# Routing and experts of a mixture-of-experts layer in one program block, with a slot table in two parts and rows scattered unscaled

## Reference, cut to what matters

```python
x = x + attn(layernorm(x))                      # 4096 tokens, DIM = 256
z = layernorm(x).reshape(-1, 256)
aff = z @ centroids.T                           # 8 experts
assign = argmax(aff, axis=1)                    # the expert of each token
alpha = sigmoid(aff[assign])
h = relu(layernorm(z, ln_g[e], ln_b[e]) @ w1[e].T + b1[e])   # 256 -> 1024, e = assign
y = z + h @ w2[e].T + b2[e]                     # 1024 -> 256
x = x + alpha * y + (1 - alpha) * z
```

## Time and profile before

| | |
|---|---|
| median of three executions | 949.11 us (947.34 to 951.23) |
| profiled execution | 948.4 us, its span 946.3 us |
| PE busy | 870.7 us, 92% of the span |
| DVE busy | 603.1 us, 64% |
| ACT busy | 534.9 us, 57% |
| POOL busy | 315.7 us, 33% |
| mean granted clock of TensorE | 0.972 |

### The profile page before, as it was taken

One profiled execution on the slowest core, in us unless ns is written; L12 is line 12 of the kernel. 1 busy time (PEld: TensorE's weight loads), 2 busy tenths in 40 slices (PEclk: granted clock), 3 DMA queues, 4 the chain that ended last, 5 costly groups with the idle time before them and its releaser, 6 DMA issues. The chain is left out here.

```text
span 946.3 us, 20352 instructions
## 1 busy us (share of the span) xinstructions
PE 870.7 (92%) x6606; PEld 517.7 (55%) x6655; DVE 603.1 (64%) x1111; ACT 534.9 (57%) x1338; POOL 315.7 (33%) x471
## 2 busy tenths in 40 slices
PE   7999869999999999999999989924999999999996
PEld 4555413333333333333333326613999999999996
DVE  5888999888888888888888306861333333323332
ACT  4667437777777877877777874661322232232221
POOL 9988644333332232232333321461111111111111
PEclk9999979999999999999999999966999999999998
DMA  7588442422521112222213207345666566656660
GB/s 263 168 255 248 143 130 96 157 69 69 169 69 47 48 49 65 69 68 69 69 56 105 90 1 240 122 165 204 211 192 210 194 197 193 219 185 199 199 212 6
DMA packets 55139, 130.68 MB, mean 138 GB/s; under 512 B 9753, under 2 KB 30874, under 8 KB 48794
## 3 DMA queue, kind: packets, MB, share of 16 engines
q1 hardware_dynamic: 49482, 108.19, 36.7%
q0 software_dynamic: 5584, 21.54, 6.0%
HBM read 101.21 MB, written 28.48 MB: 137 GB/s over the span
## 5 line engine op out<-in xcount | busy, mean ns | idle before, releaser
L802 ACT ACTIVATE arena<-ps_pair 128x512 f32<-128x512 f32 (+3 forms) x768 | 328.9, 494 | 102.2 <-PE ps_pair L1134 94.7
L891 DVE TENSOR_REDUCE B_block_max<-ps_item 128x8 f32<-128x1024 f32 x288 | 340.5, 1220 | 40.9 <-PE ps_item L1041 37.8
L1134 PE MATMUL ps_pair<-q_stack,k_stack 99*128 99x512 bf16 (+5 forms) x720 | 182.3, 330 | 12.4 <-ACT arena L802 6.8
L717 POOL TENSOR_SCALAR_AFFINE_SELECT arena<-arena 128x256 f32<-128x256 f32 x256 | 103.9, 406 | 202.6 <-ACT arena L802 200.2
L1150 PE MATMUL ps_pair<-arena,B_v_quad 128*32 128x512 f32 (+3 forms) x1536 | 163.6, 498 | 1.0 <-ACT B_oacc L816 0.7
L1134 PEld LDWEIGHTS ps_pair<-q_stack,k_stack 99*128 99x128 bf16 (+1 forms) x768 | 54.0, 97 | 187.4 <-ACT arena L802 170.2
L1686 PEld LDWEIGHTS D_ps_h<-D_xT,arena 128*128 128x128 f32 x1248 | 147.8, 195 | 4.6 <-ACT D_xT L1624 2.7
L1686 PE MATMUL D_ps_h<-D_xT,arena 128*128 128x128 f32 x1248 | 148.3, 278 | 2.1 <-ACT D_xT L1624 2.1
L1705 PE MATMUL D_ps_y<-arena,D_hr 128*128 x624 | 141.0, 379 | 0.0
L1615 ACT ACTIVATE D_hr<-D_ps_h,ffn_columns 128x128 f32<-128x128 f32 x156 | 44.5, 368 | 165.4 <-PE D_ps_h L1686 165.4
L1598 POOL DMA_INDIRECT out<-D_res,D_ids x39 | 38.4, 984 | 259.5 <-issue 200.9
(11 more groups left out here) (163 smaller groups left out, 730.6 us busy)
## 6 DMA issues: line engine op xcount, KB each, us to landing
arena<-in_w_exp SPq DMA_DIRECT2D x39, 1024.0 KB
qk_parts<-arena SPq DMA_DIRECT2D x32, 384.0 KB, 3.5
q_stack<-qk_parts SPq DMA_DIRECT2D x96, 128.0 KB, 3.0
rows<-payload SPq DMA_DIRECT2D x39, 257.0 KB, 2.7
arena<-in_x SPq DMA_DIRECT2D x16, 512.0 KB, 6.2
k_stack<-qk_parts SPq DMA_DIRECT2D x64, 128.0 KB, 3.0
arena<-in_w_exp POOLq DMA_DIRECT2D x8, 1024.0 KB, 6.8
arena<-in_x_feat SPq DMA_DIRECT2D x8, 512.0 KB, 5.8
```

Of the source, the lines that this page charges most:

```text
L717: pool.affine_select(out=block_p, in_=block_p, compare_op=ALU.is_ge, fill=0.0, base=0, pattern=[[0, 2], [1, P]], channel_multiplier=-1).th ...
L802: act.activation(pr[s % PR][:, h, 0:QW - off], ps_s[(QH * s + j) % R][:, 0:QW - off], ACT.Exp, scale=scale).then_inc(s_e, 1)
L891: dve.tensor_reduce(bmx[:, g:QH:GH, first:first + 3 * gap + 1:gap], src[:, :, :].rearrange("p c (b n) -> p c b n", n=P), AX.X, ALU.max).th ...
L1134: pe.matmul(ps_s[(QH * s + j) % R][:, 0:QW - off], ks[rows, r, half, bass.ds(g * SEQ + kb * P, P)], qs[rows, r, half, bass.ds(g * SEQ + c ...
```

## The change

The two phases become one block, so each engine runs on into the slots by itself. `GROUPS` becomes (4, 4, 4, 4, 8, 8). The first four groups (16 tiles, 2048 tokens) are counted first, and a small table for eight slots is made from them by `first_table`, on DVE behind the ninth pair of tiles: whichever way tokens fall, 2048 of them fill at least eight slots of 128 rows. SP loads rows and weights of the first slots when that table and those four groups' scatters are there. The last two groups' ranks, positions and scatters move behind the start of the slots (PE's `rank_products` in steps 0 and 1, DVE's `positions` and `row_scalars` in the same steps, POOL's 16 scatters ahead of its first store of a result), and the table of the other 31 slots is made by `rest_counts` and `rest_table` in steps 2 and 3. It is waited for in step 7, and by SP ahead of slot 8.

Rows are scattered as they are, 256 floats with five scalars (scale, shift, a factor, gate, token number): 261 floats. The writes of `pay` fall away (32 of L1323, and 32 of the residual by L1326 or L1422). Instead ACT normalizes each slot's rows (`normalize`, into `zz`, two buffers), and DVE rebuilds the residual in place (`tail`). PE transposes `zz` in place of `rows`. Working tiles of the slots lie where x lay before, and `ps_h`, `ps_x` and `ps_y` share PSUM banks with `ps_o` and `ps_p`. Row 0 of the slots is transposed ahead of the last tile's projection.

```diff
-GROUPS = (4, 8, 8, 6, 4, 2)
+GROUPS = (4, 4, 4, 4, 8, 8)
+FIRST_GROUPS = 4
+FIRST_SLOTS = 8
...
-PAYW = 2 * DIM + 2
+COL_S, COL_B, COL_K, COL_GATE, COL_ID = range(DIM, DIM + 5)
...
-                sp.wait_ge(s_fl, 32)
                 sp.wait_ge(s_tab, 2)
-                sp.wait_ge(s_zz, 2 * G)
-                sp.wait_ge(s_tl, 2 * G - tails_act(2 * G))
-                sp.wait_ge(s_tla, tails_act(2 * G))
                 load_w1(sp, Step(0))
-                for g in range(NG):
+                for g in range(FIRST_GROUPS):
                     sp.wait_ge(s_sc[g], 16 * GROUPS[g])
                 for S in range(2):
                     load_rows(sp, Step(S))
                 load_w1(sp, Step(1))
...
+                def emit(n):
+                    S = n + 2
+                    if S.reg is None and S.const == FIRST_SLOTS:
+                        sp.wait_ge(s_tab, 4)
+                        for g in range(FIRST_GROUPS, NG):
+                            sp.wait_ge(s_sc[g], 16 * GROUPS[g])
+                    if n.reg is not None or n.const >= 0:
+                        rows_of(S)
+                    if S.within(NSLOT) and (S.reg is not None or S.const >= 2):
+                        wait(sp, s_m1[1], n, 1, 1, alone=gate)
+                        load_w1(sp, S)
+                steps(sp, emit)
...
                     pool.wait_ge(s_ps, g + 1)
+                    pool.wait_ge(s_sb, 4 * (g + 1))
+                    pool.wait_ge(s_x2, starts[g + 1] // 2)
                     for t in range(starts[g], starts[g + 1]):
...
-                                                pay[:, t % RP, :], None).then_inc(s_sc[g], 16)
+                                                xr[:, t, :], None).then_inc(s_sc[g], 16)
...
-                def scaled(t):
...
-                    act.activation(pay[:, t % RP, 0:DIM], xx[t // G][:, t % G, :], ACT.Identity, bias=sd[:, 6, t:t + 1],
-                                   scale=sd[:, 5, t:t + 1]).then_inc(s_zz, 1)
-                    if by_act(t):
-                        act.activation(pay[:, t % RP, DIM:2 * DIM], xx[t // G][:, t % G, :], ACT.Identity, bias=sd[:, 8, t:t + 1],
-                                       scale=sd[:, 7, t:t + 1]).then_inc(s_tla, 1)
...
+                def normalize(S):
+                    if S.within(NSLOT):
+                        wait_dma(act, s_rl, S)
+                        wait(act, s_tx, S, 1, -1)
+                        wait(act, s_tl, S, 1, -1)
+                        row = rows[:, S.ring(RD), :]
+                        act.activation(zz[:, S.ring(2), :], row[:, 0:DIM], ACT.Identity, bias=row[:, COL_B:COL_B + 1],
+                                       scale=row[:, COL_S:COL_S + 1]).then_inc(s_zz, 1)
...
+                for g in range(FIRST_GROUPS, NG - 1):
+                    roots(g)
+                act.wait_ge(s_fl, 32)
+                act.wait_ge(s_tab, 2)
+                normalize(Step(0))
...
+                    normalize(n + 2)
+                    S = n + 1
+                    if S.within(NSLOT):
...
-                def tail(t):
-                    dve.wait_ge(s_sb, 4 * (group_of[t] + 1))
...
-                    dve.tensor_scalar(pay[:, t % RP, DIM:2 * DIM], xx[t // G][:, t % G, :], sd[:, 7, t:t + 1], sd[:, 8, t:t + 1],
-                                      ALU.mult, ALU.add).then_inc(s_tl, 1)
...
+                def row_scalars(g):
+                    dve.wait_ge(s_sd, 2 * (g + 1))
...
+                    dve.reciprocal(xr[:, of(g), COL_S], sd[:, 1, of(g)]).then_inc(s_sb, 1)
+                    dve.wait_ge(s_rs, g + 1)
+                    dve.tensor_tensor(xr[:, of(g), COL_K], sd[:, 1, of(g)], sd[:, 2, of(g)], ALU.mult).then_inc(s_sb, 1)
+                    dve.tensor_tensor(xr[:, of(g), COL_GATE], top[:, of(g)], sd[:, 2, of(g)], ALU.mult).then_inc(s_sb, 1)
+                    dve.wait_ge(s_sb, 4 * g + 1)
+                    dve.scalar_tensor_tensor(out=xr[:, of(g), COL_B], in0=mv[:, of(g), 0], scalar=-1.0, in1=xr[:, of(g), COL_S],
...
+                def first_table():
+                    F = FIRST_SLOTS
+                    totals(0, FIRST_GROUPS).then_inc(s_t1, 1)
+                    dve.wait_ge(s_t1, 1)
+                    blocks(0, 1, FT, ALU.is_ge).then_inc(s_t1, 1)
...
+                for u in range(NP):
+                    add(u)
+                    if u % 2 == 0 and 2 <= u <= 2 * FIRST_GROUPS:
+                        positions(u // 2 - 1)
+                        row_scalars(u // 2 - 1)
+                    if u % 2 == 1 and u < 2 * FIRST_GROUPS:
+                        one_hot(u // 2)
+                    if u < 2 * FIRST_GROUPS:
+                        stats(u)
+                    if u == 2 * FIRST_GROUPS:
+                        first_table()
+                    if u > 2 * FIRST_GROUPS:
+                        stats(u - 1)
+                    if u == NP - 3:
+                        one_hot(FIRST_GROUPS)
+                stats(NP - 1)
+                one_hot(NG - 1)
+                used_slots()
...
+                def tail(S):
+                    if S.within(NSLOT):
+                        row = rows[:, S.ring(RD), :]
+                        wait(dve, s_zz, S, 1, 1)
+                        dve.scalar_tensor_tensor(out=row[:, 0:DIM], in0=zz[:, S.ring(2), :], scalar=row[:, COL_K:COL_K + 1], in1=row[:, 0:DIM],
+                                                 op0=ALU.mult, op1=ALU.add).then_inc(s_tl, 1)
...
+                dve.wait_ge(s_tab, 2)
+                dve.wait_ge(s_fl, 32)
...
+                    tail(n + 1)
+                    if n.reg is None and n.const == 0:
+                        positions(FIRST_GROUPS)
+                        row_scalars(FIRST_GROUPS)
+                    if n.reg is None and n.const == 1:
+                        positions(NG - 1)
+                        row_scalars(NG - 1)
...
+                    if n.reg is None and n.const == 2:
+                        rest_counts()
+                    if n.reg is None and n.const == 3:
+                        rest_table()
...
+                def turn_rows(S):
+                    if S.within(NSLOT):
+                        wait(pe, s_zz, S, 1, 1)
...
+                        for c in range(DC):
+                            mm = pe.transpose(ps_x[:, c, :], zz[:, S.ring(2), c * P:(c + 1) * P], ident)
+                        mm.then_inc(s_tx, 1)
...
+                for n in range(-3, NT - 1):
...
+                    if t == NT - 1:
+                        turn_rows(Step(0))
+                    if t >= 0:
...
                                 mm.then_inc(s_m1[f // HC], 1)
-                    S = n + 1
-                    if S.within(NSLOT):
-                        wait_dma(pe, s_rl, S)
-                        wait(pe, s_xt, S, DC, 0)
-                        for c in range(DC):
-                            mm = pe.transpose(ps_x[:, c, :], rows[:, S.ring(RD), c * P:(c + 1) * P], ident)
-                        mm.then_inc(s_tx, 1)
+                    if n.reg is None and 0 <= n.const < NG - FIRST_GROUPS:
+                        rank_products(FIRST_GROUPS + n.const)
+                    if n.reg is not None or n.const >= 0:
+                        turn_rows(n + 1)
                     S = n + -1
```

More of the change, by code:

```diff
@@ L1183, in phase_route @@
         R = 4
+        RO = 3
         NG = len(GROUPS)
-        LAST = NG - 1
+        NP = NT // 2
         starts = [sum(GROUPS[:g]) for g in range(NG + 1)]
-        group_of = [g for g in range(NG) for _ in range(GROUPS[g])]
-        RP = 2 * G
-        assert starts[NG] == NT and all(k % 2 == 0 and k <= G for k in GROUPS)
-        xx = [a.rearrange("p (t n) -> p t n", t=G) for a in free]
+        FIRST = GROUPS[:FIRST_GROUPS]
+        FT = sum(FIRST)
+        assert starts[NG] == NT and all(k % 2 == 0 and k <= G for k in GROUPS) and all(k == 4 for k in FIRST)
+        assert (FT * P - NE * (P - 1) + P - 1) // P >= FIRST_SLOTS
+        REST = NSLOT - FIRST_SLOTS
+        xr = sb("x_rows", [P, NT, PAYW])
         oT = sb("oT", [P, R, DC, P])
-        pay = sb("pay", [P, RP, PAYW])
         st = sb("st", [P, R, 6])
         mv = sb("mv", [P, NT, 2])
-        sd = sb("sd", [P, 10, NT])
+        sd = sb("sd", [P, 3, NT])
+        eps2 = sb("eps2", [P, 1])
         top = sb("top", [P, NT])
@@ L1344, in _, with roots @@
-                for t in range(starts[LAST], NT):
-                    scaled(t)
+                def roots(g):
+                    act.wait_ge(s_v, starts[g + 1])
+                    act.activation(sd[:, 0, of(g)], mv[:, of(g), 1], ACT.Sqrt, bias=eps).then_inc(s_sd, 1)
+                    if g == 0:
+                        act.wait_ge(s_pre, 6)
+                    act.activation(sd[:, 1, of(g)], mv[:, of(g), 1], ACT.Sqrt, bias=eps2[:, :], scale=1.0 + EPS).then_inc(s_sd, 1)
+                def normalize(S):
[6 more added lines that the diff above has]
+                                       scale=row[:, COL_S:COL_S + 1]).then_inc(s_zz, 1)
@@ new lines, in _ @@
```

(25 more changed lines are left out.)

544 lines of the change are left out of this document (243 added, 301 removed).

## The result

The changed kernel takes 934.2 us (median of four executions, 933.61 to 935.95) beside 949.58 of the kernel before: a ratio of 0.9843, 95% interval 0.9817 to 0.9868. The prediction was 920.5, with 915 to 929 as its range.

The account below looks back on a forecast made before the run. PE was taken to bound the projection and slots, nothing that computes the 29.25 us between. Span 946.3 less 28.1 saved is 918.2, plus 2.1 outside 920.3; against the median 0.7 more, stated as 920.5, range 915 to 929.

Parts of the forecast that it names:

- Start of the slots: Projection to hidden(0): table and rows ready in time, hidden(0) starts at 622.35 at full clock, ending 32.6 us earlier.
- The 1.5 us at tile 22: Projection stage: PE waits 1.5 us for banks (0 to 5.4), until DVE's tenth add, delayed by first_table.
- the 0.41 that I took: Projection stage, DVE: first_table's twelve chained instructions at 0.41 us each, 4.9 in all (2.2 to 8.8).
- Rival 1: DVE later than counted, first_table at up to the old table's 8.8 us: 924 to 927, say 926; chance 0.22.
- The new wait: Ahead of hidden(1): PE idle 2.5 us for xT, behind normalize and DVE's tail; 28.4 us saved to hidden(1)'s end.
- my term: At hidden(1): the clock falls after PE's 2.5 us pause, so hidden(1) takes 6.29 us; 2.7 less without the fall.
- rival 4: No clock fall at hidden(1), PE's pause being 2.0 or less; 2.7 less, partly returned at res(2): 919.2; chance 0.13.
- Behind it: First slots: POOL's 16 scatters end at 650.8, slot 0's store lands 653.7, res(2) due 654.3: hidden by 0.6 us.
- Rival 2: First slots: scatters slowed beside busy DVE, res(2) stalls 2.8 us at 1.47 each (923), 4.8 at 1.6 (925); chance 0.08.
- Steady slots: The 33 repeated slots: cadence stays 7.25 us, row-load landings hidden up to 3.75, slack 1.05, cost 0.
- Rival 3: Every slot's row load comes onto the path: 933 to 961; chance 0.05 for over 930, 0.04 for slower than before.

Follow-up runs that it names:

- norm_later: Changed kernel with one ACT edit: in step 0 xT(1) is made ahead of normalize(2); 934.2 us, ratio 0.9827, kernel before at 949.8.
- behind: Changed kernel with all 16 late scatters in one train behind the store of slot 1; 935.2 us, ratio 0.9855, kernel before at 949.8.
- half: Changed kernel with late scatters in two trains of eight, ahead of the stores of slots 0 and 2; 919.6 us, ratio 0.9720, kernel before at 945.5.
- paced: Changed kernel with late scatters in four trains of four, ahead of the stores of slots 0 to 3; 926.1 us, ratio 0.9758, kernel before at 949.8.
- place3_half: Changed kernel with two trains of eight late scatters, rerun where the kernel before took 949.1; 927.8 us, ratio 0.9766.
- place3_thin: Changed kernel with 4, 3, 3, 3, 3 late scatters ahead of stores 0 to 4 and xT(1) ahead of normalize(2); 922.0 us, ratio 0.9711, before at 949.1.
- same_1: The changed kernel itself, unedited, rerun where the kernel before took 944.3; 924.9 us, ratio 0.9777.
- busy: Changed kernel with a POOL memset in place of each of the 16 late scatters; 918.0 us, ratio 0.9728, kernel before at 944.4.

## Why the prediction was wrong

**Start of the slots: right.** No idle time is left ahead of hidden(0), and rows and table were there. From the first projection product to hidden(0) it took 50.4 us (before, to the end of the projection, 49.4). The 1.5 us at tile 22 didn't come. What came was a fallen clock at the start of the stage, by which some products of the first tiles took longer (window 571 to 573):

```profile
571.00:573.00 2.00, 2.00 (x6) 1.47 (x6) 0.00 (x0) 0.19 (x1) 0.00 (x0) 0.52 1.03 336
```

What I mis-sized is first_table. First and last of its instructions:

```profile
599.92 0.15 DVE L1507 SCALAR_TENSOR_TENSOR C_cnt<-cst,C_seen 1x8 f32<-1x8 f32 x1
...
602.08 0.20 DVE L1548 TENSOR_TENSOR slot_tab<-C_es,cst 1x8 int32<-1x8 f32 x1
```

2.36 us for twelve, 0.20 each: near the lower bound of the sum (0.18), not the 0.41 that I took. Rival 1 falls with it. The price that I took it from, 0.55 each for the old table, had the hold in it: its rows stand beside scatters back to back (628.20 to 642.62), and DVE waits there for its own last results, 3.85 of the 8.8 us in seven waits. Two of them:

```profile
636.07 0.47 DVE L1459 TENSOR_TENSOR C_more<-C_cnt,cst 1x256 f32<-1x256 f32 x1 [1.50 <-DVE C_cnt L1456]
...
639.01 0.47 DVE L1472 TENSOR_TENSOR C_tab<-cst,C_ns 1x312 f32<-1x312 f32 x1 [0.53 <-DVE C_ns L1469]
```

first_table has the first two of four scatters beside it and no such wait.

**The new wait: right in place and size, wrong in what it costs.** 2.38 us ahead of hidden(1), ended by xT, behind normalize, behind DVE's tail, 2.5 forecast; `norm_later` moved that one normalize and left 1.04. But the clock did not fall: hidden(1) took 3.84. The pause was longer than the 2.0 after which it had fallen before; and after the same rest hidden(1) took 3.84 in `behind` and 5.46 in `half`. Two of `half`:

```profile
618.59 3.77 PE L1745 MATMUL C_bank<-arena 128*128 128x128 f32 x32
...
625.22 5.46 PE L1745 MATMUL C_bank<-arena 128*128 128x128 f32 x32 [2.38 <-ACT arena L1422]
```

So one execution keeps the clock over 2.38 us and another doesn't, and my term was a chance, not a price. The part of rival 4 on the clock came true, though not by its condition, a pause of 2.0 or less. To the end of hidden(1) the change had won 30.9 on this count; I had 28.4, or 31.1 without the clock.

**Behind it: here the prediction failed.** The step was "POOL ... issues 16 scatters, 1.26 each ... Just hidden": the train stood in the sum at nothing, as work beside which the slots run on. The train itself was as priced: 628.35 to 648.71 is 1.27 each. I asked who waits for its end (res(2), by its buffer) and priced what is queued behind it; I took for granted that PE runs at its own rate beside it. Where the kernel before stands near 949 it doesn't: 18.1 us are lost from hidden(1) to hidden(3) in place of nothing. `behind` moves this loss and `paced` and `place3_half` divide it; `place3_thin` nearly takes it away.

Where there is no hold, the train still isn't hidden. In `same_1` the store of slot 0 is issued at 652.71 (I had 650.8) and lands 5.40 later (I had 2.9), and res(2) is due at 653.2 (I had 654.3), so it waits 5.06 where I had 0.6 to spare. That costs PE 3.54, and half clock adds 2.8: a stall of the kind of rivals 2 and 4, larger than either had it by the landing. 924.9 lies inside the range, but in part by luck, since the kernel before took 944.3 there: the change gains 19.3, where 28.6 was forecast. 934.2, in the place of the result, lies outside.

The trace of before had a trace of it that I read as unexplained. Two rows of its DVE, during and just behind eight scatters back to back (613.42 to 622.29), and a piece of the chain that ended last:

```profile
621.27 0.69 DVE L1431 TENSOR_TENSOR arena<-C_ps_p,arena 128x512 f32<-128x512 f32 x1 [2.84 <-PE C_ps_p L1509]
...
624.98 0.21 DVE L1409 TENSOR_TENSOR C_rank<-C_ps_k,C_seen 128x48 f32<-128x48 f32 x1 [1.50 <-remote]
```
```profile
623.34 1.62 another core or an unknown queue
```

PE's ranks for the second stand at 619.2 in its timeline, over 5 us before DVE may read them. PE had nothing to do behind its last projection, but the chain goes through DVE here, so the kernel before paid for these waits as well, some 4 us by my estimate (2.84 + 1.50). It would fit the 4 to 5 us by which the kernel before is shorter in places without the hold; no trace of it was taken there. The change puts a train twice as long beside the slots.

**The end: not seen.** 2.7 us more between the last store and the end of the span, with the same store and nothing behind it. It is in each profile of the one-block program that I compared (in `same_1` too, from its last store's issue to its end). The traces have it in POOL's last instruction, the drain at the end of the block. It takes 3.24 us before, where the block issued 39 indirect transfers, 4.56 in `busy` with 55, and 5.86 with 71 in every other run. Both differences are 0.08 for each indirect transfer more, and 32 of them make 2.6.

**Steady slots: right.** 7.25 from one hidden to the next, and 265.9 in all, before and after. Rival 3 had nothing: row loads of 130.5 KB land sooner than those of 257 (2.5/2.7/2.9). From 690 to 880 us:

```profile
DMA to landing us min/median/max: 2.0/2.1/2.2
```

Rival 2's price didn't come either: from 628.35 to 648.71 the scatters keep 1.27 each. The one long one among them stands beside DVE's new tail:

```profile
630.87 1.15 POOL L1342 DMA_INDIRECT payload<-C_x_rows,C_posi  x1 [0.30 <-issue]
```
```profile
630.71 0.47 DVE L1620 SCALAR_TENSOR_TENSOR rows<-arena,rows 128x256 f32<-128x256 f32 x1
```

It takes 1.15 in place of 0.96, and `same_1` has the same pair (a scatter of 1.15 at 634.80, a tail at 634.64). The contention that the Trainium skill, page "SBUF — State Buffer", section "Who interferes with whom", states for a DVE instruction with two SBUF inputs and a GpSimd instruction that reads SBUF fits this row. It is worth 0.2 us in a train of 20, and not every tail does it: the one at 650.15 in `same_1` leaves the scatter at 650.18 at 0.96.

**What stays open.** Why PE is held. It needs the indirect scatters or POOL's work for them in a long row (the bytes are excluded; `busy`, which would have parted the scatters from a POOL that is merely busy, met a place without the hold), and it needs the place. What differs between the places no run here shows. Nor was a train tried beside the loop: every late one stands beside the first steps, which each engine's program has written out (the loop starts with step 8), so a shortage of instructions under a train is not excluded.

## What to carry to other kernels

A long train of indirect scatters is not a cost of POOL alone. Split it so that POOL rests between three or four, and look at whether the engines beside it get their signals when their rows say. Where DVE or ACT is released microseconds after the row that it waits for, another engine's train is a suspect. A price read from rows beside such a train has the hold in it. And have the kernel under study itself in every group of experiments: four runs here looked like cures and were in a place without the hold.

## What the runs showed of the hardware that was not expected

- PE can be held, and its signals delivered 10 to 16 us late, while POOL issues indirect scatters 1.27 us apart; with rows of 20 bytes as with 1044. DVE's signals to itself come late as well (1.50 in the trace of before), and SP issues slowly (0.69 in place of 0.34). Shown in three groups of runs with the kernel before at 949.1 to 949.8, absent in two groups at 945.5 and 944.3 that had long trains. One chip number stands over a group of each kind.
- POOL's drain at the end of a block takes longer the more indirect transfers the block issued: 3.24 us with 39, 4.56 with 55, 5.86 with 71.
- TensorE's clock stayed at its full level over a rest of 2.38 us in some executions (hidden(1) 3.84) and fell after the same rest in others (5.46); over one of 3.54 it fell (6.38).
- Twelve chained instructions of DVE on one partition, 8 to 128 elements wide, take 0.20 us each where no hold is on.
